# A quantized transformer block on one core: the rows of the first attention group behind the last down product, the last query projections inside that group, and TensorE summing the fourth key tile in every second group

## The reference

```
q    = qdq(layernorm(x)) @ qdq(wq).T + bq        # rows rounded to 255 levels
k, v = split(ctx @ wkv.T + bkv)
attn = softmax(q k^T / sqrt(32))                 # 512 x 512 for each of 4 batches x 16 heads
x    = x + tanh(g) * (qdq(attn v) @ qdq(wp).T + bp)
```

## Time and profile before

| | |
|---|---|
| median of 3 runs | 924.2 us (923.75 to 928.88) |
| the profiled execution | 926.07 us |
| its span, first to last instruction | 924.3 us |
| mean granted TensorE clock | 0.956 of full |
| PE, DVE, ACT, POOL busy over the span | 87%, 82%, 62%, 60% |
| POOL busy from about 580 to 808 us | nearly all the time |

### The profile page before, as it was taken

How to read it: one execution, slowest core, us unless ns; L and a number is a source line. 1 busy time by engine, 2 the same in 40 slices (tenths; PEclk the granted TensorE clock), 3 DMA queues, 4 the chain that set the end, 5 groups by cost and what they waited for, 6 DMA issues and landing times.

```text
span 924.3 us, 14336 instructions
## 1 busy us (share of the span) xinstructions
PE 804.3 (87%) x4253; PEld 348.2 (38%) x4253; DVE 756.2 (82%) x1462; ACT 573.7 (62%) x974; POOL 558.2 (60%) x636
## 2 busy tenths in 40 slices
PE   4898997689899999899999978999999999865663
PEld 3444543334344444444444432223232323222221
DVE  5999999789898999899888768778888888525884
ACT  5888896444476555666555554666666666646762
POOL 7867753142334344344444344999999999946671
PEclk9999999899999999999999996999999999977986
DMA  9998975433352353354334372431313130000111
GB/s 308 273 238 211 223 209 151 120 73 65 67 116 58 74 125 64 75 84 84 80 70 78 60 164 54 104 92 48 91 48 90 49 89 5 2 1 0 61 53 69
DMA packets 186986, 90.70 MB, mean 98 GB/s; under 512 B 138641, under 2 KB 171553, under 8 KB 186913
## 3 DMA queue, kind: packets, MB, share of 16 engines
q1 hardware_dynamic: 186592, 89.82, 40.5%
q10 hardware_dynamic: 320, 0.01, 0.0%
HBM read 44.05 MB, written 16.78 MB: 66 GB/s over the span
## 4 chain that ended last, share of the span: by engine, by line
PE 37%; DVE 34%; issue 13%; ACT 9%; POOL 3%; DMA 2%; SPq 1%; DVEq 0%; ACTq 0%; POOLq 0%
PE bank L1144 11%; PE bank L1236 5%; PE bank L1156 5%; PE bank L1226 4%; PE bank L1207 4%; DVE bank L1570 3%; POOL B L690 3%; DVE gsm L1572 3%; DVE B L1581 3%; DVE B L1696 3%; DVE B L1575 2%; PE bank L1354 2%; ACT bank L844 2%; ACT A L971 2%; PE bank L1248 1%
## 5 line engine op out<-in xcount | busy, mean ns | idle before, releaser
L1144 PE MATMUL bank<-A,B 128*128 128x512 f16 x1024 | 232.6, 380 | 13.1 <-DVE B L1581 13.1
L621 POOL TENSOR_TENSOR B<-B 128x512 f16<-128x512 f32 x64 | 75.7, 1184 | 215.3 <-DVE B L1581 133.9
L1696 DVE TENSOR_REDUCE B<-bank 128x1 f32<-128x512 f32 x256 | 161.5, 682 | 42.4 <-PE bank L1207 42.3
L971 ACT ACTIVATE A<-bank 128x512 f32<-128x512 f32 x256 | 142.7, 602 | 84.5 <-PE bank L1226 82.6
L690 POOL TENSOR_TENSOR B<-B,A 128x512 f32<-128x512 f32 x124 | 160.1, 1327 | 0.0
L1144 PEld LDWEIGHTS bank<-A,B 128*128 128x128 f16 x1024 | 99.2, 98 | 138.6 <-DVE B L1581 16.4
L1156 PE MATMUL bank<-A,B 128*128 128x512 f16 x512 | 120.7, 379 | 0.0
L844 ACT ACTIVATE bank<-B 128x512 f32<-128x512 f32 x64 | 38.5, 601 | 130.6 <-DVE B L1575 130.6
L1226 PE MATMUL bank<-A 98*128 98x512 f16 x256 | 97.3, 393 | 9.5 <-ACT A L971 7.9
L1207 PE MATMUL bank<-A 96*128 96x512 f16 x256 | 99.1, 403 | 5.7 <-DVE B L1696 4.1
L690 POOL TENSOR_TENSOR B<-A 128x512 f32<-128x512 f32 x64 | 79.9, 1271 | 14.4 <-ACT A L971 14.0
(11 more groups left out here) (214 smaller groups left out, 1465.0 us busy)
## 6 DMA issues: line engine op xcount, KB each, us to landing
B<-in_L_ffn_w_dram SPq DMA_DIRECT2D x48, 256.0 KB, 3.7
A<-k_parts SPq DMA_DIRECT2D x48, 128.0 KB, 2.5
A<-q_parts SPq DMA_DIRECT2D x48, 128.0 KB, 3.6
X<-in_x_dram SPq DMA_DIRECT2D x4, 1024.0 KB, 8.8
B<-in_ctx_dram SPq DMA_DIRECT2D x16, 256.0 KB, 6.4
k_parts<-B SPq DMA_DIRECT2D x16, 256.0 KB, 4.5
v_rows<-B SPq DMA_DIRECT2D x16, 256.0 KB, 3.2
q_parts<-B SPq DMA_DIRECT2D x32, 128.0 KB
```

Source lines behind the costliest of these rows:

```text
L621: nc.gpsimd.tensor_tensor(HLb[j][:, 1, :], Db[j % 2], HLb[j][:, 0, :], ALU.subtract).then_inc(lo_done, 1)
L971: nc.scalar.activation(PR[(HG * t + j) % 8], bank[2 + j % 2][:, :], ACT.Exp, scale=SCALE).then_inc(exp_done, 1)
L1144: last = mm(bank[2 * n + q][:, :], XQT[a][:, m, :], wt[:, m % DB, j * 512:j * 512 + 512], start=(m == 0), stop=(m == 2 * DB - 1))
L1696: reduce(NMX[g % 2][:, t, j:j + 1], bank[ROW_BANKS[r % 3]][:, :], AX.X, ALU.max, negate=True).then_inc(row_max, 1)
```

## The change

Three things are changed.

The **order before attention**. The first rows of group 0 come right behind the last down product; q_project of tile 13 comes behind three of them, q_turn of tile 14 behind six, and the other ten rows follow. DVE takes q_max of tile 15 behind the first three maxima and q_full of tile 13 behind eight. POOL sets the ones under the keys (ones_under) earlier and all in one go.

The **last query steps inside group 0**. q_project of tile 14 goes into slot 2 of group 0, q_turn of tile 15 into slot 4, q_project of tile 15 into slot 7; on DVE q_ints of tile 15 into slot 3, q_full of tile 14 into slot 5 and of tile 15 into slot 10; on ACT q_operands of tile 15 behind slot 5, q_bias of tile 14 behind slot 7 and of tile 15 behind slot 13; on POOL q_low of tile 14 behind the first four adds and q_low of tile 15 ahead of the adds of group 1. SP stores tiles 14 and 15 in group 1.

The **sums**. In every odd group POOL leaves out the adds of the fourth key tile, so that it makes eight and not twelve (the last group, 15, is odd and had eight before). sum_last is issued in slot 3 of the next (even) group, and sum_weights in slot 5 adds to it. ACC takes other memory: of the four buffers that the even groups had, they keep two and take XQT for the others; the odd groups get the other two and WQT.

```diff
--- before.py
+++ after.py
@@ -27,6 +27,11 @@
 WUP = 256.0
 LN_EPS = 1e-5
+def adds_before(b, g):
+    return b * 40 + g * 12 - g // 2 * 4
@@ -185,8 +190,10 @@
         used[0] = 0
         OALL = part(TOK * D, F32, "p (t d) -> p t d", t=TOK)
-        ACC = [[part(SEQ, F32) for _ in range(HG)],
-               [a.bitcast(F32).rearrange("p n t -> p (n t)") for a in XQT] + [a.rearrange("p k t -> p (k t)") for a in (QF, QB)]]
+        low = [part(SEQ, F32) for _ in range(HG)]
+        wq_halves = WQT[:, :, :].rearrange("p k d -> p (k d)").bitcast(F32).rearrange("p (h s) -> p h s", h=2)
+        ACC = [low[0:2] + [a.bitcast(F32).rearrange("p n t -> p (n t)") for a in XQT],
+               low[2:4] + [wq_halves[:, h, :] for h in range(2)]]
         assert used[0] <= 20480
@@ -494,9 +501,8 @@
             send_c(0, 0)
             send_c(0, 1)
-            for u in range(TOK - DB - 1, TOK):
+            for u in range(TOK - DB - 1, TOK - 2):
                 store_q(u)
-            sp.wait_ge(q_out, 32 * TOK)
@@ -506,6 +512,10 @@
                     if not (first and g == 0 or last and g == DB - 1):
                         send_c(*following(b, g))
+                    if first and g == 1:
+                        store_q(TOK - 2)
+                        store_q(TOK - 1)
+                        sp.wait_ge(q_out, 32 * TOK)
@@ -660,35 +670,42 @@
                 pool.wait_ge(b_ps, FC * TOK)
-                pool.wait_ge(diag3, TOK)
                 if g > 0:
-                    pool.wait_ge(q_lo, TOK - DB + 1 + g)
+                    pool.wait_ge(ks_ones, g)
                 nc.gpsimd.memset(KS[96:98, HG * g:HG * g + HG, :], 1.0).then_inc(ks_ones, 1)
-                pool.wait_ge(ks_ones, g + 1)
...
             q_rstd(TOK - 2)
             q_low(TOK - 4)
+            pool.wait_ge(q_lo, TOK - 3)
+            ones_under(0)
+            pool.wait_ge(ks_ones, 1)
             q_diag(TOK - 2)
             q_rstd(TOK - 1)
             q_diag(TOK - 1)
-            ones_under(0)
-            for u in (TOK - 3, TOK - 2, TOK - 1):
-                q_low(u)
-                ones_under(u - TOK + 4)
+            pool.wait_ge(diag3, TOK)
+            for g in range(1, DB):
+                ones_under(g)
+            pool.wait_ge(ks_ones, DB)
+            q_low(TOK - 3)
...
                 for g in range(DB):
                     n, acc = b * DB + g, ACC[g % 2]
-                    for t in range(1, TB - 1 if last and g == DB - 1 else TB):
+                    if first and g == 1:
+                        q_low(TOK - 1)
+                        pool.wait_ge(qp_ps, TOK)
+                    for t in range(1, TB - 1 if g % 2 else TB):
                         for j in range(HG):
...
                                 up_to(pool, sum_ps, n - 1)
                             else:
-                                pool.wait_ge(acc_done, n * 12 + HG * (t - 2) + j + 1)
+                                pool.wait_ge(acc_done, adds_before(b, g) + HG * (t - 2) + j + 1)
                             nc.gpsimd.tensor_tensor(acc[j], PR[j] if t == 1 else acc[j], PR[(HG * t + j) % 8],
                                                     ALU.add).then_inc(acc_done, 1)
+                        if first and g == 0 and t == 1:
+                            q_low(TOK - 2)
@@ -932,9 +949,6 @@
             q_round(TOK - 1)
             q_bias(TOK - 3)
-            q_operands(TOK - 1)
-            q_bias(TOK - 2)
-            q_bias(TOK - 1)
@@ -966,7 +980,7 @@
                         up_to(act, pv_tile, n * TB + t - 1)
                         for j in range(HG):
-                            up_to(act, acc_done, n * 12 + (j - 7, j - 3, j + 1, j + 1)[t])
+                            up_to(act, acc_done, adds_before(b, g) + (j - 7 if g % 2 else j - 3, j - 3 if g % 2 else 0, j + 1, j + 1)[t])
                             act.wait_ge(st_ps, n * 16 + HG * t + j + 1)
@@ -976,6 +990,12 @@
                             if (t, j) == (2, 1) and not closing:
                                 c_out(*following(b, g))
+                            if (t, j) == (1, 1) and opening:
+                                q_operands(TOK - 1)
+                            if (t, j) == (1, 3) and opening:
+                                q_bias(TOK - 2)
+                            if (t, j) == (3, 1) and opening:
+                                q_bias(TOK - 1)
@@ -1161,6 +1181,9 @@
                 pe.wait_ge(li3, u + 1)
                 up_to(pe, lt_out, u)
+                if u == TOK - 1:
+                    pe.wait_ge(ct_ready, 1)
+                    pe.wait_ge(ct_low, 1)
                 for k in range(DB):
@@ -1210,6 +1233,8 @@
                 n = b * DB + g
                 pe.wait_ge(row_max, n * 16 + 16)
+                if n < 2:
+                    pe.wait_ge(lt_out, TOK - 1 + n)
                 up_to(pe, den_ready, n - 2)
@@ -1237,15 +1262,17 @@
                 last_.then_inc(pv_tile, 1)
-            def sum_weights(b, g, final=False):
+            def sum_weights(b, g):
                 n = b * DB + g
-                pe.wait_ge(acc_done, n * 12 + (8 if final else 12))
-                if not final:
+                pe.wait_ge(acc_done, adds_before(b, g) + (8 if g % 2 else 12))
+                if n == 0:
+                    pe.wait_ge(qf_ready, TOK)
+                if g % 2 == 0:
                     up_to(pe, sm_ready, n)
                     up_to(pe, o_norm, n)
                 for j in range(HG):
-                    last_ = mm(bank[7][DH * j:DH * j + DH, :], ones[:, 0:DH], ACC[g % 2][j], start=not final, stop=True)
+                    last_ = mm(bank[7][DH * j:DH * j + DH, :], ones[:, 0:DH], ACC[g % 2][j], start=g % 2 == 0, stop=True)
                 last_.then_inc(sum_ps, 1)
@@ -1292,6 +1319,14 @@
                         if slot == 1 and not opening:
                             weigh(*preceding(b, g), TB - 1)
+                        if slot == 2 and opening:
+                            q_project(TOK - 2)
+                        if slot == 4 and opening:
+                            q_turn(TOK - 1)
+                        if slot == 7 and opening:
+                            q_project(TOK - 1)
+                        if slot == 3 and g % 2 == 0 and not opening:
+                            sum_last(*preceding(b, g))
                         if slot == 5 and not opening:
@@ -1311,20 +1346,15 @@
             down(TOK - 1, 2, 1)
             down(TOK - 1, 3, 1)
-            q_project(TOK - 3)
-            q_turn(TOK - 2)
             pe.wait_ge(d_done, FC * TOK)
             pe.wait_ge(down_read, TOK - 1)
             first_rows(0, 3)
-            q_project(TOK - 2)
-            first_rows(3, 5)
-            q_turn(TOK - 1)
-            first_rows(5, 8)
-            q_project(TOK - 1)
-            first_rows(8, 16)
+            q_project(TOK - 3)
+            first_rows(3, 6)
+            q_turn(TOK - 2)
+            first_rows(6, 16)
             pe.wait_ge(down_read, TOK)
             pe.wait_ge(h_done, FC * TOK)
-            pe.wait_ge(qf_ready, TOK)
             c_turn(0, 0)
@@ -1332,7 +1362,7 @@
             weigh(BATCH - 1, DB - 1, TB - 1)
             sum_last(BATCH - 1, DB - 1)
-            sum_weights(BATCH - 1, DB - 1, True)
+            sum_weights(BATCH - 1, DB - 1)
             sum_turn(BATCH - 1, DB - 1)
@@ -1729,6 +1759,12 @@
                         if slot == 12:
                             bias_row(b * DB + g)
+                        if slot == 3 and opening:
+                            q_ints(TOK - 1)
+                        if slot == 5 and opening:
+                            q_full(TOK - 2)
+                        if slot == 10 and opening:
+                            q_full(TOK - 1)
                         if slot == 14 and not opening:
@@ -1751,15 +1787,12 @@
             q_stats(TOK - 1)
             q_ints(TOK - 2)
-            q_full(TOK - 3)
             link(ts(LSC, LSC, 1.0 / 127.0, None, ALU.mult))
             ts(LSC, LSC, TG[:, 3:4], None, ALU.mult).then_inc(area_free, 1)
+            first_maxima(0, 3)
             q_max(TOK - 1)
-            first_maxima(0, 2)
-            q_full(TOK - 2)
-            q_ints(TOK - 1)
-            first_maxima(2, 8)
-            q_full(TOK - 1)
+            first_maxima(3, 8)
+            q_full(TOK - 3)
             first_maxima(8, 16)
             maxima(0, 1, 0)
             c_low(0, 0)
```

## The result

The changed kernel takes 933.7 us (median of 4 runs, 932.17 to 935.26), the kernel before 924.0 in the same session (923.49 to 928.88). The ratio of the two is 1.0074 with the interval [1.0046, 1.0102]: 6.8 us slower (4.2 to 9.4), inside the 1% that I had called "no change" and with the sign that I gave. The medians of these few runs lie 9.7 us apart; I go by the ratio. In size it is about three times the +2.1 of my sum. The profiled execution is 932.42 us, of which 930.7 is span.

A forecast was written before the change was run, and what follows sets the result against it. PE and DVE, not the nearly full POOL, were taken to bound attention. Opening -0.1 (-3.9, 3.8 given back) and seven sum_last +2.2 made +2.1 us: 928.2 profiled, 926.3 us as median, range 920 to 931.

The forecast's parts named there:

- What bounds attention: Groups 1 to 12: the chain runs through PE and DVE, POOL is led; removing 28 adds gains nothing.
- sum_last at +0.32 us each: Slot 3 of seven even groups: weigh moves 0.32 us later, bounds 0 and 0.86 each; +2.2 us in all.
- The order before attention at -3.9: Before group 0: DVE's last maximum ends at 560.25 instead of 564.11, so first scores come 3.9 us earlier.
- The steps inside group 0, S + 25.0: Group 0's sum comes 25.0 us after first scores S, against S + 21.2 before; 3.8 us given back.
- my marker: Sum of group 0 starts within 1.5 us of 590.8, released by PE or ACT and not by POOL.
- The opening's sum: Order before attention and steps inside group 0 together: 3.8 us given back of 3.9 gained, -0.1 us.
- q_low of tile 15 ahead of group 1's adds, "at most 0.1": On POOL: delays the fourth exponential of group 1's third key tile by at most 0.1 us, with 1.1 in hand.
- sum_last at full price: Rival, 15%: PE has no hole in slots 3 to 5, PE and DVE delay each other; 7 x 0.86, 930.1 us.
- The tail: Sum of group 14 starts some 2 us later than 808.5 and still waits for POOL.
- POOL as the pace: Rival, 14%: POOL sets the groups' pace, odd ones shorten by 0.65 us, even ones lose 0.2; 920.9 us.
- The opening keeps its gain: Rival, 8%: clock up at first scores and q_bias finds ACT idle; -3.9 + 2.2 = -1.7, 922.5 us.
- The relief doesn't happen: Rival without its own chance: exponentials waiting for adds keep POOL's pace; same time as the forecast.

The follow-up runs named there:

- experiment 1: The kernel before, with eight POOL adds in every odd group and nothing summing their fourth key tile, except in the last group; ratio 0.9987 [0.9968, 1.0005].
- experiment 3: The changed kernel with twelve POOL adds in all groups but the last and no sum_last in slot 3; ratio to the kernel before 1.0105 [1.0074, 1.0136].
- 9: The kernel before with only the sums changed, and each sum_last in slot 3 issued twice; one run, 938.43 us.
- 4: The changed kernel with DVE's bias row of group 1 moved from slot 12 to slot 15; ratio to the kernel before 1.0062 [1.0043, 1.0081].
- 6: The kernel before plus one POOL instruction ahead of the adds of group 2 (full width) and group 3 (half width); one run, 934.96 us.
- 8: The kernel before plus a half-width POOL instruction ahead of group 2's adds, no wait changed; one run, 936.47 us.
- Experiment 7: The kernel before plus a full-width POOL instruction ahead of group 2's adds, whose fifth add waits for an exponential two later; one run, 927.52 us.

## Why the prediction was right or wrong

**What bounds attention** (PE and DVE; the relief of POOL costed at nothing): right, shown by experiment 1 within 0.01 us a period. The adds that were 0.36 us early were the evidence that decided it, not the 98% busy.

**sum_last at +0.32 us each**: right in mechanism, too small in size. That weigh, and not the maxima, carries it, that DVE loses nothing, and that ACT's copy hides part of it, all hold; the term measured 0.65, and 4.4 for the seven. What was missing are 0.32 us of issue time at the ends of blocks of quadrant products between products that run one at a time (0.09 + 0.14 at sum_last, 0.09 ahead of weigh). I had taken the block's 0.86 from rows in which it stands next to its like the earlier trace rows. The price was to be seen in the trace before, in other slots than the one I read: in slot 1 of group 9 weigh starts 0.31 behind the scores, where half-precision products follow each other 0.22 apart, and the next row starts 0.99 behind weigh.

```profile
709.50 0.38 PE L1226 MATMUL bank<-A 98*128 98x512 f16 x1
709.81 1.06 PE L1236 MATMUL bank<-A,B 128*32 128x512 f32 x8
710.80 0.65 PE L1207 MATMUL bank<-A 96*128 96x512 f16 x2
```

My bounds of 0 to 0.86 held it.

**The order before attention at -3.9**: -4.9 in the trace. The order of the work was right, and the maxima, not PE, set it. The surplus of 1.0 is what the first row gains, 0.9 us: it starts 3.73 us behind the last down product, against 4.65 before (548.42 less 543.77), where I had left it in place. From the first row to the last maximum it takes 11.64 us, where I had 11.83. In the eight profiles with the old opening the last maximum comes 20.3 to 20.4 us behind the last down product, whether the first row comes 4.1 or 5.3 behind it; in the five with the new one it comes 11.63 to 11.64 behind the first row. Why the first row comes earlier (3.4 to 3.8) isn't shown.

**The steps inside group 0, S + 25.0**: S + 25.06, but not by the path that I gave, and that the two agree so closely is partly luck. Weigh's part came as planned: PE was free of it at 591.96, S + 24.9. But POOL, planned to end at S + 24.35, ended at 592.05, S + 25.0, and released the sum, against my marker. Its eight adds took 10.84 us and not 10.3, since one of them took 2.25 beside the bias row of group 0: the same exclusion as in group 1, at POOL's cost, and missing from the plan here too. The opening's sum is -0.7 to -1.3 and not -0.1, all of the difference from the step before.

**q_low of tile 15 ahead of group 1's adds, "at most 0.1"**: this is the step that failed. I asked who waits for POOL's results and found 1.1 us in hand. That part was nearly right: the exponential of slot 11 in group 1 does wait for POOL, and starts 0.30 behind the end of its scores in place of 0.10, 0.2 us late where I had said 0.1 at most; whether any of it is in the 2.7 isn't shown. I didn't ask what POOL's occupancy does to an instruction that waits for none of them. It used up the moment in which POOL waits in each group, and DVE's bias row, which shares SBUF with POOL's adds, couldn't run until they ended: 2.7 us here, 8.6 with twelve adds (experiment 3). It is the largest single error in the sum. ACT's timeline of the kernel after, the exponentials of slots 11 to 13 and the wait for POOL ahead of them:

```profile
598.25 1.74 ACT L985 ACTIVATE A<-bank 128x512 f32<-128x512 f32 x3 [0.26 <-POOL WQT L705]
```

**The number.** The forecast was 926.3 in a range of 920 to 931. The ratio makes 931.0 of the 924.2 it was counted from, just the upper end; the median of 933.7 lies above it. That end was made for sum_last at full price and a spread of the runs, and not for what happened, so that its being reached and not clearly passed is luck.

**The tail**: the sum of group 14 waits for POOL, 1.28 us (1.27 before), as said.

**The rivals.** POOL as the pace: fallen (1). The opening keeps its gain: fallen, 0.7 to 1.3 of 4.9. sum_last at full price because PE and DVE make each other late: its time of 930.1 was close, but its mechanism is fallen (9), and what filled the gap were two other things. The relief doesn't happen: it does, 4.9 to 5.5 us of idle time for each group, worth nothing.

**The rule of the lock**, as far as the runs go. In all thirteen profiles I took, for each of the 16 bias rows, the last instruction of POOL ahead of it that had really waited (started 0.08 us behind the end of what released it, in two cases 0.14). In 203 of the 208 such a wait lay at most 7.5 us back (at most six adds), and the row took 0.67 to 1.08 us. In the five others (group 1 of after and of experiments 3 and 4, group 2 of 6 and 8) there was none in the 18.9 us ahead, and they are the five locked ones. Experiment 7 has the backlog of 6 with one wait added, and belongs to the 203. My first idea, that it matters whether the *next* add finds its input there long before, falls: for the add that was next when the row asked, it had been there for 1.4 to 2.9 us in groups 1 and 2 that weren't locked (2.9 in experiment 7) and for 1.7 to 3.0 in those that were. This is a rule read off the runs, and only experiment 7 changes the wait alone. What stays open is where between 7.5 and 18.9 us the limit lies, and why a wait matters at all; neither was tried.

## What to carry to other kernels

An engine that is 98% busy but is led by another is no bound, and freeing it gives nothing; yet its short waits can be what lets a neighbour into SBUF, so an instruction that is put ahead of a nearly full stream on POOL should be priced by what DVE does with two SBUF operands under that stream, not only by who waits for POOL's results. Where a block of quadrant products is moved between products that run one at a time, its price is the distance from the product before to the product behind it at such a place, not the block's own time. And before a difference of two traces is laid to a change, take off what lies ahead of the changed code: here a third of it.

## What the runs showed of the hardware

- A DVE addition with two SBUF operands (128 x 512), mostly 1.07 us, took 1.77, 4.75, 8.64, 9.63 and 9.81 us when POOL ran additions beside it and hadn't waited for anything in the 18.9 us ahead; each time it ended 0.54 to 0.56 us after POOL's last instruction. With one wait of POOL in the 7.5 us ahead, even one too short to be seen as idle time, it took 0.67 to 1.08.
- The other way round, POOL's pair of additions beside such a row took 2.94 us in place of 2.50, and beside the row of group 0, which took 0.67, one addition took 2.25 in place of 1.27.
- A block of eight quadrant products, 0.85 to 0.88 us next to its like, takes 0.99 to 1.00 to a next product outside the quadrants, of half or full precision, and 0.09 to enter. Between half- and full-precision products that both run one at a time no such time is seen (0.22 and 0.11, the plain spacings).
- When a lock left PE idle for 6.67 us, the granted clock fell to its lower level for 6.8 us behind it, and weigh took 1.94 us in place of 1.06.
- The first products of the program start at 14.64 us in one profile and at 16.4 to 16.8 in twelve, with the same code, and the last period of attention takes 10.9 us at a granted clock of 1.00 and 15.7 at 0.50, whatever the version. The two together are as large as what this change does.
